# Gated layer: the states of two groups turned in a row every second slot, into two PSUM banks

## The reference

```python
def step(h, _):
    m_in = jnp.einsum('nm,bmd->bnd', in_matrix, h)      # in_matrix = out_matrix = adj
    m_out = jnp.einsum('nm,bmd->bnd', out_matrix, h)
    av = jnp.concatenate([m_in, m_out], axis=-1)
    u3 = h @ u3_w.T + u3_b
    z = jax.nn.sigmoid(av @ w3_w.T + w3_b + u3)
    r = jax.nn.sigmoid(av @ w4_w.T + w4_b + u3)
    hv = jnp.tanh(av @ w5_w.T + w5_b + (r * h @ u5_w.T + u5_b))
    h = (1.0 - z) * h + z * hv
    return (h, None)
h, _ = jax.lax.scan(step, input, None, length=5)
```

## Time and profile before

| | us |
|---|---|
| median of 3 runs | 1387.19 (1386.95 to 1387.49) |
| the profiled execution, its own time | 1387.39 |
| its span in the trace | 1385.2 |
| PE busy | 1349.8, 97% of the span |
| DVE / ACT / POOL busy | 1108.6 / 927.9 / 753.7 |
| first and last turn of the gated layer begin | 183.7 / 975.6 |

### The profile page before, as it was taken

The page is one execution under the profiler, slowest core; times in us unless marked ns, Lnnn a source line. Parts: engine busy times, 40 slices in busy tenths (PEclk is TensorE's granted clock), DMA queues, the critical chain, the costliest instruction groups (busy, mean ns, idle before and its releaser), DMA issues.

```text
span 1385.2 us, 26908 instructions
## 1 busy us (share of the span) xinstructions
PE 1349.8 (97%) x8470; PEld 1184.3 (85%) x8470; DVE 1108.6 (80%) x2632; ACT 927.9 (67%) x1666; POOL 753.7 (54%) x745
## 2 busy tenths in 40 slices
PE   9999979999999999999999999999889999999995
PEld 7888868888888888888888888887689999999994
DVE  5888878777778777778777787777688888888885
ACT  5666647677777776777777777766546666666664
POOL 4111127666666666666666666665435555555553
PEclk9999999999999999999999999999999999999998
DMA  3222232000021000020000110000212222222211
GB/s 107 96 92 91 96 103 77 1 0 0 9 82 32 0 0 0 30 83 8 0 0 0 46 46 1 0 0 8 76 54 70 70 68 68 68 68 68 68 39 38
DMA packets 60041, 61.16 MB, mean 44 GB/s; under 512 B 4691, under 2 KB 39381, under 8 KB 59989
## 3 DMA queue, kind: packets, MB, share of 16 engines
q1 hardware_dynamic: 59556, 60.31, 13.6%
q10 hardware_dynamic: 432, 0.20, 0.1%
HBM read 35.33 MB, written 25.17 MB: 44 GB/s over the span
## 4 chain that ended last, share of the span: by engine, by line
PE 94%; DVE 3%; ACT 2%; issue 1%; POOL 0%; ACTq 0%; POOLq 0%; DVEq 0%
PE psum L969 6%; PE psum L663 5%; PE psum L665 5%; PE psum L651 5%; PE psum L346 4%; PE psum L365 4%; PE psum L981 3%; PE psum L983 3%; PE psum L706 3%; PE psum L695 3%; PE psum L678 3%; PE psum L707 3%; PE psum L676 3%; PE psum L696 3%; PE psum L699 3%; PE psum L698 3%
## 5 line engine op out<-in xcount | busy, mean ns | idle before, releaser
L626 POOL TENSOR_TENSOR rh_lo<-rh,rh_hi 128x512 fp32r<-128x512 f32 x160 | 207.1, 1294 | 265.6 <-ACT rh_hi L741 265.6
L632 POOL TENSOR_TENSOR h_lo<-h,h_hi 128x512 fp32r<-128x512 f32 x160 | 216.6, 1354 | 12.8
L741 ACT CAST rh_hi<-rh 128x512 fp32r<-128x512 f32 x160 | 99.4, 621 | 149.2 <-DVE rh L773 149.2
L754 DVE TENSOR_TENSOR psum<-psum,h 128x512 f32<-128x512 f32 x160 | 111.9, 699 | 103.5 <-ACT psum L745 103.5
L663 PE MATMUL psum<-adj_t_hi,hn_hi 128*128 128x256 f32 x640 | 172.1, 303 | 1.0 <-DVE m_lo L767 1.0
L738 ACT ACTIVATE psum<-psum,bias_cols 128x512 f32<-128x512 f32 x160 | 106.8, 667 | 80.1 <-PE psum L683 80.0
L665 PE MATMUL psum<-adj_t_hi,hn_lo 128*128 128x256 f32 x640 | 158.9, 282 | 0.0
L773 DVE TENSOR_TENSOR rh<-psum,h 128x512 f32<-128x512 f32 x160 | 110.1, 688 | 50.3 <-ACT psum L738 50.2
L663 PEld LDWEIGHTS psum<-adj_t_hi,hn_hi 128*128 128x128 f32 x640 | 121.8, 190 | 1.9 <-issue 1.8
L665 PEld LDWEIGHTS psum<-adj_t_hi,hn_lo 128*128 128x128 f32 x640 | 122.2, 191 | 0.0
L728 ACT ACTIVATE z<-psum,bias_cols 128x512 f32<-128x512 f32 x160 | 111.3, 695 | 0.0
(11 more groups left out here) (184 smaller groups left out, 4119.8 us busy)
## 6 DMA issues: line engine op xcount, KB each, us to landing
x_in<-in_x_dram SPq DMA_DIRECT2D x32, 256.0 KB, 2.8
x_dram<-x SPq DMA_DIRECT2D x32, 256.0 KB, 2.1
g_x<-x_dram SPq DMA_DIRECT2D x32, 256.0 KB, 3.3
h_dram<-h SPq DMA_DIRECT2D x32, 256.0 KB, 2.0
ht<-h_dram SPq DMA_DIRECT2D x32, 256.0 KB, 2.9
c_x<-x_dram SPq DMA_DIRECT2D x32, 256.0 KB, 3.1
out_dram<-res SPq DMA_DIRECT2D x32, 256.0 KB, 2.4
conv_in<-in_L_gnn_weight_dram SPq DMA_DIRECT2D x1, 448.0 KB, 4.8
```

The source lines that it names most:

```text
L626: pool.tensor_tensor(rh_lo[:, q, :], rh[:, q, :], rh_hi[:, q, :].bitcast(F32), ALU.subtract).then_inc(rh_lo_done, 1)
L632: pool.tensor_tensor(h_lo[:, q, :], h[:, (g - 1) % G, :], h_hi[:, q, :].bitcast(F32), ALU.subtract).then_inc(h_lo_done, 1)
L754: dve.tensor_tensor(cb, cb, hg, ALU.subtract).then_inc(dif_done, 1)
```

## The change

In slots 8 to 151 the turns go in pairs. In an even slot PE turns the states of g and then at once those of g + 1; in an odd slot it turns nothing. The odd group's turn goes to bank 7 (B_HN_ODD), and ACT and DVE read the bank through `hn_bank`. The wait on hn_lo_done asks for s - 1 in place of s where g > 1. Slots 0 to 7 and 152 to 159 keep a turn in every slot, into bank 0. The convolution layers, which use bank 7 next, wait once for hn_lo_done to reach 152 (pairs_end).

```diff
--- before.py
+++ after.py
@@ -540,7 +540,7 @@
     rh_lo = sb("rh_lo", [128, 2, COLS], F32R)
     z = sb("z", [128, 2, COLS])
 
-    B_HN, B_M, B_R, B_GATE = 0, 1, 2, 4
+    B_HN, B_M, B_R, B_GATE, B_HN_ODD = 0, 1, 2, 4, 7
     B_CAND = (3, 6)
 
     x1_loaded = [sem(f"x1_loaded{i}") for i in range(G)]
@@ -580,6 +580,13 @@
 
         return not isinstance(base, int) or 0 <= base + g - lag < SLOTS
 
+    def paired(base, g):
+
+        return not isinstance(base, int) or G <= base + g < SLOTS - G
+
+    def hn_bank(base, g):
+        return B_HN_ODD if paired(base, g) and g % 2 else B_HN
+
     earlier = {}
 
     def sync(sp):
@@ -635,21 +642,30 @@
         yield from run(pool, slot, 3)
 
     def tensor(pe):
+        def turn(base, g, k, bank):
+
+            s = base + g
+            if k is not None:
+                pe.wait_ge(x1_loaded[g], k * 16 + 16)
+            else:
+                pe.wait_ge(h_done, s - G + 1)
+
+            wait_count(pe, hn_lo_done, s - 1 if paired(base, g) and g > 1 else s)
+            if isinstance(base, int) and s == 0:
+                pe.wait_ge(earlier["xt_done"], GROUPS)
+            for i in range(TILES):
+                src = x1[:, g, i, :] if k is not None else h[:, g, i * 128:(i + 1) * 128]
+                mm = pe.transpose(psum[:, bank, i * 128:(i + 1) * 128], src, ident[:, :])
+            mm.then_inc(hn_mm, 1)
+
         def slot(base, g, k):
             s = base + g
-            if live(base, g, 0):
-
-                if k is not None:
-                    pe.wait_ge(x1_loaded[g], k * 16 + 16)
-                else:
-                    pe.wait_ge(h_done, s - G + 1)
-                wait_count(pe, hn_lo_done, s)
-                if isinstance(base, int) and s == 0:
-                    pe.wait_ge(earlier["xt_done"], GROUPS)
-                for i in range(TILES):
-                    src = x1[:, g, i, :] if k is not None else h[:, g, i * 128:(i + 1) * 128]
-                    mm = pe.transpose(psum[:, B_HN, i * 128:(i + 1) * 128], src, ident[:, :])
-                mm.then_inc(hn_mm, 1)
+            if not paired(base, g):
+                if live(base, g, 0):
+                    turn(base, g, k, B_HN)
+            elif g % 2 == 0:
+                turn(base, g, k, B_HN)
+                turn(base, g + 1, k, B_HN_ODD)
             if live(base, g, 1):
 
                 p = (g - 1) % 2
@@ -718,10 +734,10 @@
                 if k is not None:
                     if not (isinstance(k, int) and k == 0):
                         act.wait_ge(h_out[g], k * 16)
-                    act.copy(h[:, g, :], psum[:, B_HN, :])
+                    act.copy(h[:, g, :], psum[:, hn_bank(base, g), :])
                     act.copy(hn_hi[:, g % 2, :, :], x1[:, g, :, :]).then_inc(hn_hi_done, 1)
                 else:
-                    act.copy(hn_hi[:, g % 2, :, :].rearrange("p i d -> p (i d)"), psum[:, B_HN, :]).then_inc(hn_hi_done, 1)
+                    act.copy(hn_hi[:, g % 2, :, :].rearrange("p i d -> p (i d)"), psum[:, hn_bank(base, g), :]).then_inc(hn_hi_done, 1)
             if live(base, g, 3):
                 act.wait_ge(z_mm, s - 2)
                 wait_count(act, inc_done, s - 4)
@@ -754,7 +770,7 @@
                 dve.tensor_tensor(cb, cb, hg, ALU.subtract).then_inc(dif_done, 1)
             if live(base, g, 0):
                 dve.wait_ge(hn_hi_done, s + 1)
-                src = x1[:, g, :, :].rearrange("p i d -> p (i d)") if k is not None else psum[:, B_HN, :]
+                src = x1[:, g, :, :].rearrange("p i d -> p (i d)") if k is not None else psum[:, hn_bank(base, g), :]
                 dve.tensor_tensor(hn_lo[:, g % 2, :, :].rearrange("p i d -> p (i d)"), src,
                                   hn_hi[:, g % 2, :, :].rearrange("p i d -> p (i d)").bitcast(F32),
                                   ALU.subtract).then_inc(hn_lo_done, 1)
@@ -779,7 +795,7 @@
 
     programs = {"sync": sync, "gpsimd": gpsimd, "tensor": tensor, "scalar": scalar, "vector": vector}
     sems = {"h_out": h_out, "hn_lo_done": hn_lo_done, "m_lo_done": m_lo_done, "z_done": z_done,
-            "rh_done": rh_done, "h_done": h_done, "slots": SLOTS}
+            "rh_done": rh_done, "h_done": h_done, "slots": SLOTS, "pairs_end": SLOTS - G}
     return programs, (earlier, sems)
 
 
@@ -1014,6 +1030,8 @@
 
                 pe.wait_ge(y1_loaded[u % 2], it * (32 * U // 2) + 32 * (u // 2 + 1))
                 wait_count(pe, y1_done, s)
+                if isinstance(it, int) and s == 0:
+                    pe.wait_ge(earlier["hn_lo_done"], earlier["pairs_end"])
                 if isinstance(it, int) and s == 2:
                     pe.wait_ge(x2t_lo_done, 1)
                 for b in range(GB):
```

## The result

| | before | after |
|---|---|---|
| median, us (5 runs each) | 1387.26 (1386.95 to 1387.96) | 1425.11 (1422.61 to 1426.43) |
| ratio | | 1.0272, 95% interval 1.0258 to 1.0286 |
| span of the profiled execution, us | 1385.2 | 1423.2 |
| from the turn of slot 8 to the turn of slot 152, us | 702.77 | 743.20 |

The changed kernel is 2.7% slower, 37.9 us. The forecast was 1430.8 us, 43.6 us more than before, with a range of 1418 to 1449.

A forecast was written before the change was run, and what follows sets the result against it. The prediction took PE's always busy queue to bound the stage. To 1387.2 us it added 36.8 us of pauses and 6.8 us of clock falls, with nothing saved by pairs: 1430.8 us, range 1418 to 1449.

The forecast's parts named there:

- The bound: In the stage from 233.9 to 950 us PE is always busy, so every microsecond it stands lengthens the run.
- The wait: Once per block, 18 times, PE stands before the first pair's odd turn: 1.74, 2.47 or 2.58 us, 36.8 us in all.
- my row: Trace row of the kernel before: 0.15 us from DVE's end of its subtraction to the start of a waiting turn.
- The clock: Pauses also lower PE's clock: four falls of 1.7 us among the 18 pauses, 6.8 us, bounds 0 and 30.6 us.
- Rival 1: PE's clock falls at every one of the 18 pauses, 30.6 us, giving 1454.6 us; chance 0.09.
- What a pair saves: Putting two turns in a row on PE, 72 pairs in slots 8 to 151, saves zero; at most 5.8 us.
- My upper bound of 5.8 us: Most the pairs could save: 72 pairs times the 0.08 us that shows behind a turn.
- the 0.08 us behind the turn: Extra distance on PE after a turn's first adjacency matmul: 0.20 us to its successor where the next is 0.12 us.
- The sum: 36.8 us of pauses plus 6.8 us of clock falls less 0 for the pairs, 43.6 us more than before.
- Rival 2: ACT and DVE run ahead after a pause, PE's 18 waits of 6.6 us vanish, no fall: 1417.4 us; chance 0.03.
- Rival 3: Faster: the first pair's wait is met when PE comes to it and each pair saves 0.08 us: 1381.4 us; chance 0.02.
- The argument that the wait cannot be met before DVE is done: DVE's subtraction ends at the shortest 2.03 us after the turn's start, where 0.44 us would be needed to avoid waiting.

The follow-up runs named there:

- run 1: Changed kernel, but the odd turn of each block's first pair asks for one hn_lo_done count less; 1379.63 us, ratio 0.9955.
- run 2: Kernel before plus only PE's wait for hn_lo_done of the same slot, behind the first turn of each of 18 blocks; 1428.38 us, ratio 1.0314.
- run 3: Changed kernel, all waits kept, but the odd turn moved behind the even slot's reset gate matmuls; 1382.79 us, ratio 0.9976.
- run 4: Changed kernel with six unused 512-column matmuls put into each of the 18 pauses between the two turns; 1416.95 us, ratio 1.0222.
- runs 5 to 7: Second bank, a turn in every slot, old waits; the same with looser wait; kernel before without the turn's h_done wait: ratios 1.0001, 0.9996, 1.0000.
- run 8: Kernel before with each turn done twice over in place, eight transposes in a row in one bank; 1441.48 us, ratio 1.0405.

## Why the prediction was right, and where it was off

**The bound.** That the stage is as long as PE's queue was right. All 18 pauses lengthened it one for one: an ordinary block took 40.27 us against 38.40 us in run 1, which is the 1.68 us of the pause and 0.19 us of slower matmuls. Over the stage the changed kernel is 743.20 - 696.20 = 47.0 us longer than run 1: 35.7 us of pauses, 9 us of clock falls, 2 us of slower matmuls.

**The wait.** That the odd turn of the first pair waits for its own pair's even turn, that it does so once in each of 18 blocks and in no other pair, and that the length can be read from the trace of before was right, and runs 1, 2 and 3 show it from three sides. The size: the second turn came 2.12 us after the first in ordinary blocks (2.18 forecast), 2.81, 2.82 and 2.92 us at a set's beginning (2.91) and 2.92 to 2.94 us behind it (3.02). Less 0.44 us each, that is 11 x 1.68 + 7.2 + 10.0 = 35.7 us, against 36.8. The 1.1 us come from the delay from DVE's end to PE's start: 730.32 + 0.68 to 731.06 is 0.06 us, not the 0.15 of the earlier trace rows. It was 0.06 in 17 of the 18 pauses and 0.15 in one. Less 0.04 us in each ordinary block, since DVE ended 2.06 us after the turn and not 2.02, that gives the difference. The 50 to 100 ns for reading a semaphore that the Trainium skill states (Advanced Engine Details and Errata, Network/Comms) were nearer than my row; I had weighed them, at 1.3 us less, and kept to the row.

**The clock.** I had counted three falls at the seven long pauses and one at the eleven short ones, 6.8 us. In the profile there were six at the long ones and none at the short ones, 9.0 us by run 4. Outside the stage the profiled execution of the changed kernel was 2.4 us quicker than before's; both of the falls that before had ahead of 222 us (at 196.7 and 206.9) were missing in it. That a pause of 2.3 us brings a fall in six of seven cases here and in one of seven in run 2 says that its number is not to be forecast from the pauses' length. Rival 1 (a fall at every pause) is wrong for the 11 ordinary ones, none of which had one. The page of the Trainium skill that it leaned on (TensorE: Matmul & The Clock Gate, A second HAM failure mode: psum-queue depth-cycling) is borne out at six of the seven long pauses here and at one of seven in run 2, and at no short one.

**What a pair saves.** This was the term that failed: "I take a saving of zero". Run 1 measures the saving at 6.8 us in time and 6.57 us in the stage. The transposes are 0.11 us apart in the row of eight, as I had said, and a row of eight costs what two rows of four do. But I had looked for the gain only at the turn itself, and counted the gate matmuls as fixed. They were not: they run 1 to 2% closer. The trace of before had the hint, since two equal slots in turn took 4.84 and 4.88 us with no wait in either. My upper bound of 5.8 us was too low for run 1, and that it came near is luck: it was taken from the 0.08 us behind the turn, which did not change. In the changed kernel itself the saving is less than in run 1, because in ten of the eleven ordinary blocks the second pair runs at the old pace: 40.27 us a block, where 38.88 + 1.68 = 40.56 would be no saving and 38.40 + 1.68 = 40.08 all of it.

**The sum** for the stage: 35.7 (pauses) + 9.0 (falls) - 4.3 (closer matmuls) = 40.4, as measured (743.20 - 702.77). The 4.3 us are what is left when the other two are taken out; run 1's 6.57 less the 2 us of slower matmuls gives about the same. With 2.4 us less outside, 38.0 us in the span. Forecast were 36.8 + 6.8 - 0. Two errors, 2 us in the falls and 4 us in the pairs, stood against each other, so that the forecast came within 6 us is in part luck; and the 2.4 us outside the stage are chance.

**Rival 2** (a lead of ACT and DVE pays) is out: from slot 8 to slot 152 the weight loads' waits for L738 (L754 after) went from 5.8 to 4.0 us, not to zero, and they were 4.5 us in run 1 too, where no pause gives a lead. **Rival 3** had one half right: the pairs do save, and with the wait met the kernel is faster, 1379.6 us. But that takes another program, run 1. The argument that the wait cannot be met before DVE is done held.

## What to carry to other kernels

When two steps are put in a row on an in-order queue, ask of each wait of the second whether what it waits for comes from the first: here a count that was one too high turned a gain of 0.5% into a loss of 2.7%. The length of such a pause can be read from the trace of before, as the way from the first step to the event that is waited for, and here, where the queue is the bound, it cost its full length and at some pauses a clock fall on top. And an engine that is always busy is not always equally fast: compare the same row of instructions in neighbouring slots before taking its time as fixed.

## What the runs showed of the hardware that was not expected

The same 14 distances of 512-column matmuls at full clock took 3.27, 3.23 or 3.20 us (0.2335 to 0.2288 us for one) with the same operands and no wait. One row of four transposes between the last gate matmul and the adjacency matmuls goes with the two slower values, in turn from slot to slot (kernel before, runs 5 to 7). A row of eight in the same place goes with the fast one in runs 1 and 8, but not always: in the changed kernel one pair in four ran at the slower values in ten of eleven ordinary blocks. The second PSUM bank, the looser wait with it and one wait fewer change nothing. The cause is not known.

Six matmuls that nobody needs, put into each of the 18 pauses of PE, went with no fall of its clock in the stage, where there had been six, and the kernel was faster: ratio 1.0222 to before in place of 1.0272. Pauses of about the same length (2.2 to 2.4 us idle) were followed by a fall in six of seven cases in the changed kernel and in one of seven in run 2.
